# Two waits of GpSimd inside each batch of gathers, in a graph attention and neighbour-max kernel

## What is computed

```
h = max(layernorm(x), 0)
Wh = (h @ W).reshape(N, 4, 32)
e[i,j,head] = leaky(s_src[i,head] + s_dst[j,head])      # only where adj[i,j] > 0
x = x + elu( softmax_j(e) @ Wh )
h = max(layernorm(x), 0)
x = x + max over the neighbours j of i of h[j]          # 0 for a row without neighbours
```

## Time and profile before

| | us |
|---|---|
| median of 3 runs | 625.61 |
| lowest and highest run | 618.42, 634.14 |
| profiled execution, its time | 619.35 |
| profiled execution, its span (first to last instruction) | 617.6 |
| busy: PE, DVE, ACT, POOL | 348.8, 350.5, 154.7, 332.1 |
| gathers of stage one on POOL: first and last start | 45.7, 350.3 |
| gathers of stage two on POOL: first and last start | 382.4, 590.2 |

### The profile page before, as it was taken

How to read it: one execution, slowest core, us unless ns; L and a number is a source line. 1 busy time by engine, 2 the same in 40 slices (tenths; PEclk the granted TensorE clock), 3 DMA queues, 4 the chain that set the end, 5 groups by cost and what they waited for, 6 DMA issues and landing times. The chain is left out here.

```text
span 617.6 us, 8203 instructions
## 1 busy us (share of the span) xinstructions
PE 348.8 (56%) x2410; PEld 258.7 (42%) x2410; DVE 350.5 (57%) x1375; ACT 154.7 (25%) x429; POOL 332.1 (54%) x360
## 2 busy tenths in 40 slices
PE   1847667592939385461707371511755666566764
PEld 1732334361617153251707370301643554455553
DVE  7976767772928284572818656311644554454575
ACT  1731312321314142432413242100111111121122
POOL 7927075254555637274563703774665666666620
PEclk9958588697878879595856696555677667666578
DMA  8938999994979869127120401121121122222211
GB/s 294 418 127 314 399 357 402 364 377 145 369 237 382 296 247 339 50 57 287 41 55 10 136 26 51 52 55 34 47 53 47 48 59 57 55 57 64 61 39 33
DMA packets 28740, 100.97 MB, mean 163 GB/s; under 512 B 6869, under 2 KB 13397, under 8 KB 20501
## 3 DMA queue, kind: packets, MB, share of 16 engines
q1 hardware_dynamic: 16245, 76.33, 31.8%
q0 software_dynamic: 9344, 19.75, 13.1%
q10 hardware_dynamic: 3104, 4.33, 1.9%
HBM read 93.92 MB, written 6.46 MB: 163 GB/s over the span
## 5 line engine op out<-in xcount | busy, mean ns | idle before, releaser
L711 POOL DMA_INDIRECT G<-wh_table,idx x146 | 149.3, 1022 | 112.2 <-DVE idx L1266 70.8
L1481 POOL DMA_INDIRECT G<-h_table,idx x146 | 137.8, 944 | 75.9 <-issue 35.5
L1546 DVE TENSOR_TENSOR_SCAN S<-adjf,S,psf 128x128 f32<-128x128 bf16 x107 | 51.0, 477 | 83.8 <-remote 38.7
L1513 PE MATMUL psf<-identf,S 128*128 128x128 f32 x146 | 58.1, 398 | 71.5 <-issue 53.7
L1522 PE MATMUL psf<-Sb,OL 128*128 128x128 f32 x292 | 85.2, 389 | 19.3 <-issue 12.2
L1493 ACT COPY Sb<-psf 128x128 f32<-128x128 f32 x146 | 37.4, 266 | 194.3 <-PE psf L1513 86.7
L883 PE MATMUL psf<-adjf,packw 128*128 128x512 f16 x256 | 75.1, 437 | 16.2 <-DMA adjf<-in_adj_dram 13.7
L1522 PEld LDWEIGHTS psf<-Sb,OL 128*128 128x128 f32 x292 | 67.3, 285 | 28.7 <-issue 19.8
L1513 PEld LDWEIGHTS psf<-identf,S 128*128 128x128 f32 x146 | 28.4, 195 | 86.5 <-issue 63.5
L1507 PE MATMUL psf<-identf,G 128*128 128x128 f32 x146 | 54.8, 375 | 6.6 <-DMA G<-h_table,idx 5.2
L961 PE MATMUL psf<-Xb,Rm 128*128 128x24 bf16 (+3 forms) x292 | 14.1, 185 | 71.8 <-DVE Rm L1216 71.8
(11 more groups left out here) (165 smaller groups left out, 564.9 us busy)
## 6 DMA issues: line engine op xcount, KB each, us to landing
adjf<-in_adj_dram SPq DMA_DIRECT2D x64, 1024.0 KB
adjf<-keep_table SPq DMA_DIRECT2D x4, 960.0 KB
G<-wh_table,idx POOLq DMA_INDIRECT x146
G<-h_table,idx POOLq DMA_INDIRECT x146
out_dram<-rows_out SPq DMA_DIRECT2D x32, 64.0 KB
wh_table<-OQ ACTq DMA_DIRECT2D x7, 272.0 KB, 8.5
h_table<-h1b ACTq DMA_DIRECT2D x3, 384.0 KB
xsf<-in_x_dram SPq DMA_DIRECT2D x2, 512.0 KB, 9.7
```

The lines of the kernel that those rows point to most:

```text
L711: pool.indirect_dma_start(G[:, plan.at[k] + b, :], None, wh_table, bass.IndirectOffsetOnAxis(ap=idx[:, n:n + 1], axis=0)).then_inc(gathere ...
L1481: pool.indirect_dma_start(G1[:, n % NG, :], None, h1_table, bass.IndirectOffsetOnAxis(ap=idx[:, n:n + 1], axis=0)).then_inc(found[n % NG], 16)
L1513: nc.tensor.transpose(ps[:, BACK[m % 3], 0:P], S[:, m % 5, :], ident[:, :]).then_inc(back_done, 1)
L1546: V.tensor_tensor_scan(S[:, n % 5, :], flags[:, n * P:(n + 1) * P], ps[:, n % 3, 0:P], start, ALU.mult, ALU.max).then_inc(scan_done, 1)
```

## The change

While GpSimd issues the gathers of a batch k, it now stops twice. Ahead of the eighth gather (b == 7) it waits until PE has done `scores_by_row` of the batch before (k-1). Ahead of the thirteenth (b == 12), which only batches with more than 12 blocks have, it waits until PE has done `max_back` of the batch before. The first wait is in batches 1 to 9, the second in batches 3 to 8. Nothing else changes: the same gathers in the same order, and every other engine has the same instructions.

```diff
                     for b in range(plan.size[k]):
                         n = plan.block0[k] + b
+                        if b == 7 and k:
+
+                            pool.wait_ge(rowe_done, k)
+                        if b == 12 and plan.whole(k - 1):
+
+                            pool.wait_ge(mback_done, k - 1)
                         pool.indirect_dma_start(G[:, plan.at[k] + b, :], None, wh_table,
                                                 bass.IndirectOffsetOnAxis(ap=idx[:, n:n + 1], axis=0)
                                                 ).then_inc(gathered[k % 2], 16)
```

## The result

The changed kernel takes 587.66 us (median of 4 runs, 583.46 to 590.09), beside 624.23 us for the kernel before in the same comparison (4 runs, 618.42 to 634.14): a ratio of 0.9436, with a 95% interval of 0.934 to 0.9533. The ratios of this document leave out runs more than 1.5% above the fastest of the same kernel (here the one of 634.14), so they are not exactly the quotients of the medians. The profiled execution took 583.46 us; its span is 581.9 us, 35.7 less than the 617.6 of before.

A forecast was written before the change was run, and what follows sets the result against it. DVE was taken to stand still because PE's signals are seen late during long gather runs. Savings of 11.3 and 15.6 us, 26.9 in all, took 619.35 to 592.5; half the run gap added gave 595.6 us, range 577 to 620.

The forecast's parts named there:

- A pause doesn't release anything: Rival: `em` and `dq` stay late in stage one, late gathers add 2.4 us; 622 to 628 us, chance 0.11.
- the stall moves on to the selection: Rival: signals stay late while any gather is in flight, stalling `meta`; 8.9 us gained, 613.6 us median, chance 0.20.
- The term for 15 blocks: Batches 3, 4, 5: release moves from the last gather to the twelfth, saving 3.75 us per batch, 11.3 us in all.
- the rival in which the stalls go altogether: Two pauses keep every run short, so gathers set stage one's steps; saves 53 us, 569 us median, chance 0.13.
- The term for 18 blocks: Batches 6, 7, 8: release six gathers sooner, 7.5 us less a 2.3 us pause; 5.2 us per batch, 15.6 in all.
- `meta` on time, cost 0: DVE's wait for PE's `select`, beside the at most six gathers behind the second wait: signal counted on time, cost 0.
- "slower" rival: Late gathers delay `meta`'s signal from `select` by 11.3 us; batches of 18 lose 6.1 us each; 641 us median, chance 0.08.

The follow-up runs named there:

- the computation: Changed kernel with both waits for PE replaced by a small useless GpSimd computation: 582.2 us, ratio 0.9184 to the kernel before.
- the narrow kernel: Kernel before, no pauses, each stage-one gather bringing 32 bytes a row instead of 544 (attention results wrong): 521.73 and 522.34 us, ratios 1.0005 and 1.0018.

## Why the prediction was right, and where not

**The mechanism** held. The forecast was that PE's signals are seen late beside a long run of gathers and that a pause frees them. The changed kernel shows `em` of batch 3's gathers 1.33 and `dq` of batch 7's 2.97 us after PE's end where they were 12.63 and 11.23; the kernel with a useless computation shows that a pause does it without any tie to PE; and each single wait helps its own signal most. "A pause doesn't release anything" falls, and so does "the stall moves on to the selection": `meta` has 3.8 us of remote waits in the whole stage.

**When a signal comes free** was described too simply. The prediction let it come free some 3.6 us after the last gather before a pause or the run's end, and counted it as on time in a short run. Neither is general. In the kernel before, beside batch 8's gathers, PE's scores end at 301.33 + 4.23 = 305.56 and `em` starts 9.24 us later, between two gathers of a run whose last starts at 321.38:

```profile
301.33 4.23 PE L985 MATMUL psf<-E,OQ 128*128 128x64 f32 x36
...
314.80 0.56 DVE L1294 TENSOR_TENSOR em<-psf,valid 128x384 f32<-128x384 f32 x1 [8.16 <-remote]
315.13 0.94 POOL L711 DMA_INDIRECT G<-wh_table,idx  x1 [0.30 <-issue]
```

And in the changed kernel `dq` is still 2.5 to 3.0 us late in each of the batches 3 to 8, with no run longer than seven where both waits stop, and in batch 7, where the second doesn't, in the middle of a run. So it isn't shown how much of `dq`'s gain in the batches with 18 blocks belongs to the second pause and how much to the shorter run behind the first; that the second wait alone leaves `dq` no such wait shows that it can do it alone.

**What the changed profile was to show.** `em`, `dq` and `mid` from 75 to under 45 us: 16.8. `dq` within 4 us of the start of the twelfth gather: 2.18 us in batch 3 (142.60 to 144.78) and 0.74 in batch 7. GpSimd's waits of 2 to 4 us, nine and six at most: 7 and 5, but mostly shorter, 0.9 to 1.5 us, as at 137.60 and 144.94. The pause was priced from the release seen 3.6 us after the last gather's start; in the short runs now it comes 2.2 us after in batch 3.

**The term for 15 blocks was mis-sized.** It was 3.75 us per batch, and the steps show 7.1: 3 x 3.35 = 10 us too little in the sum, more than the whole miss of 595.6 - 587.7 = 7.9. The text named the reason and didn't take it: with the first wait `em` comes in a fresh run. From `idx` to `em` it now takes 137.44 - 126.49 = 10.95 us, where it took 149.50 - 127.38 = 22.1. The 3.75 priced the second wait alone. The trace with the second wait alone, from another chip, is 16.8 us ahead at `idx` of batch 9, less than half of what both save, which is in keeping with this. For 15 blocks the step of 26.0 us lies between the 29.5 of the forecast and the 23.9 of the rival in which the stalls go altogether, and somewhat nearer to the latter.

**The term for 18 blocks was right in size,** 5.2 forecast and 4.9 measured, yet made of other parts: batch 7's first pause was 4.17 us, not 2.3, because PE's scores weren't done at the eighth gather. In the kernel before they ended 273.03 - 263.37 = 9.7 us after the first gather's start; now the gathers start sooner against them, 248.43 - 235.34 = 13.1 us. A wait for another engine's work was priced at where that work stood before, and the change moved it. That the computation, which doesn't wait for that work, reached 0.9184 on its chip is in keeping with this; the two were not timed on the same chip.

**`meta` on time, cost 0:** nearly. It has a remote wait of 2.4 us and one of 1.3, and one of 3.90 us in batch 7's step that is for PE's work. In stage one the "slower" rival had its mechanism, at about a fifth of its price (2.4 us against 11.3).

**Stage two** kept its time, as forecast (233.4 and 235.2 us).

**What no part of the prediction had** is that all of it holds for some chips only. Put side by side, from the traces:

| | `idx` of batch 9 at | first gather of stage two to the end |
|---|---|---|
| before, 617.6 us | 335.25 | 235.2 |
| changed, 581.9 us | 298.31 | 233.4 |
| computation, 579.4 us | 288.0 | 237.7 |
| changed, prompt chip, 518.1 us | 278.72 | 193.1 |

The late signals cost the kernel before 335.25 - 278.72 = 56.5 us up to batch 9, by the changed kernel's trace from a prompt chip, on which it takes the same time as the kernel before. The change gives back 37 of them and the computation 47, the latter by a trace from a third chip. That the whole 56.5 us are due to late signals is inferred, not shown. The rest of the difference between chips is in stage two, 235.2 - 193.1 = 42 us, and neither touches it.

The Trainium skill, page "SBUF — State Buffer", section "SBUF: two separate sides", says that DMA and compute don't slow each other. It speaks of the ports of the memory, not of signals between engines. Carried over to these signals, as the prediction did, it fits the traces of the prompt chips, where `dq` is 0.10 us late beside gathers, and not those of the late chips.

**Open.** What makes a chip of one kind or the other isn't known; no run changes it. No chip was timed in two groups, so it may as well be the hour as the chip, for instance what its other cores were doing. The kernel before was never traced on a prompt chip: that its signals are on time there is taken from its time and from the traces of the narrow and the changed kernel. Whether the gathers act through their bytes or through their issue was not tried where it matters, since the narrow kernel never ran on a late chip. By what path a PE signal is held up, no view shows. And neither the computation kernel by itself on a prompt chip nor one with pauses in stage two on a late chip was run; on the prompt chip, pauses in both stages cost 8.5%.

## What to carry to other kernels

A "remote" or "unknown queue" wait in a kernel on one core was here the mark of a signal that is seen late, but its length is not the lateness: measure from the end of the work waited for to the start of the waiter, and look at what runs beside it. If it is a long run of indirect gathers, try one short useless operation of their engine in the middle of it, ahead of any wait for another engine, since a wait also pays for that engine's unfinished work. And before such a cure is kept, run it on more than one chip, each time beside the kernel before: here it is worth 5.6% on one and nothing on another, and a denser set of pauses costs 1 to 9% there.

## What the chips showed that I had not expected

- The kernel before takes 520.84 and 521.34 us on two chips (medians of 13 and 19 runs) and 634.69 and 625.09 on two others (7 and 13 runs), without an instruction changed; the ranges don't touch. Between the two traces of the changed kernel each engine's busy time differs by 7 us at most (PE 363.7 and 356.7), at a mean granted clock of 0.740 on the prompt chip and 0.726 on the late one; the span differs by 63.8 us.
- On a late chip a signal from PE was seen by DVE up to 14.5 us after DVE had become ready (15.1 after PE's end), beside gathers of GpSimd, and 0.04 us after PE's end when they were over the earlier trace rows.
- Stage two has such waits too: the remote waits of `S` are 59.4 us in the changed kernel and between 45.2 and 67.0 in the lists above of the other late traces, although GpSimd stops in stage two 37 times by itself in the changed kernel (27 times for PE, 29.9 us, and 10 times remote, 9.4 us). Such pauses alone are no cure there.
